# Two attentions of a transformer stack on TensorE: score and mask matmuls in smaller array tiles, masking in the contraction, and a new call order

## The reference

```python
# x: (8, 256, 128); everything float32
x = x + layernorm(attn(layernorm(x)))     # 16 heads of 8, 4 key/value heads, causal over 256 tokens
x = x + layernorm(ffn(layernorm(x)))      # two layers of local attention and a gated MLP
# attn: q = x@Wqa@Wqb, k/v = x@Wkva@Wkvb, rope on q and k
scores = jnp.einsum('bqhd,bkhd->bhqk', q, k) * scale
scores = jnp.where(causal, -jnp.inf, scores)
out = jnp.einsum('bhqk,bkhd->bqhd', softmax(scores), v) @ Wout + bout
# each layer of ffn: 8 heads of 64, window 64; token shift, l2norm of q and k, xpos rotation
sim = jnp.einsum('bhwid,bhwjd->bhwij', q, k)          # 64 queries against 128 keys
mask = (i < j) | (i > j + 64) | (j == -1)
x = x + (softmax(where(mask, -max, sim)) @ v) @ wo
x = x + (a * gelu(g)) @ w2 + b2                        # a, g = split(layernorm(shift(x)) @ w1 + b1)
```

## Time and profile before

| | us |
|---|---|
| median of 3 runs (lowest, highest) | 502.34 (502.02, 503.59) |
| the profiled execution, its own time | 504.87 |
| its span, first to last instruction | 503.0 |
| PE busy | 467.1 (93%) |
| DVE busy | 376.5 (75%) |
| ACT busy | 343.7 (68%) |
| POOL busy | 317.0 (63%) |

### The profile page before, as it was taken

How to read it: one execution, slowest core, us unless ns; L and a number is a source line. 1 busy time by engine, 2 the same in 40 slices (tenths; PEclk the granted TensorE clock), 3 DMA queues, 4 the chain that set the end, 5 groups by cost and what they waited for, 6 DMA issues and landing times.

```text
span 503.0 us, 14088 instructions
## 1 busy us (share of the span) xinstructions
PE 467.1 (93%) x5472; PEld 292.8 (58%) x5472; DVE 376.5 (75%) x725; ACT 343.7 (68%) x906; POOL 317.0 (63%) x250
## 2 busy tenths in 40 slices
PE   8879999999999898999799989999999899999992
PEld 6555766675664566756545656655654466556641
DVE  3835684678775986899868796958888879868576
ACT  1135656565567788878886797788674888998632
POOL 2322251445979899779989865868669966564011
PEclk9979999999999989999999989999999999999996
DMA  5022022000001001010000010100010001011002
GB/s 149 2 91 89 7 45 46 4 3 3 4 2 44 3 1 22 3 43 3 1 22 2 22 23 1 24 1 22 3 22 21 20 5 23 2 23 22 2 8 76
DMA packets 13453, 11.43 MB, mean 23 GB/s; under 512 B 4194, under 2 KB 10700, under 8 KB 13388
## 3 DMA queue, kind: packets, MB, share of 16 engines
q1 hardware_dynamic: 13388, 10.54, 8.3%
HBM read 5.16 MB, written 1.05 MB: 12 GB/s over the span
## 4 chain that ended last, share of the span: by engine, by line
PE 71%; ACT 9%; DVE 8%; issue 6%; POOL 5%; DMA 1%; SPq 0%; ACTq 0%; DVEq 0%; POOLq 0%
PE bank L464 10%; PE bank L558 8%; PE bank L679 7%; PE bank L638 5%; ACT bank L1268 5%; PE bank L648 5%; PE bank L567 5%; PE bank L500 4%; PE bank L693 4%; PE bank L619 4%; PE bank L578 3%; PE bank L477 3%; PE bank L596 3%; PE bank L600 2%; POOL r_qk L2346 2%
## 5 line engine op out<-in xcount | busy, mean ns | idle before, releaser
L2346 POOL TENSOR_TENSOR r_qk<-ss,minus_half 128x16 f32<-128x16 f32 x32 | 93.7, 2929 | 2.7
L1268 ACT ACTIVATE bank<-bank,mn_b 128x128 f32<-128x128 f32 x256 | 88.8, 368 | 4.1 <-DVE mn_b L1818 4.0
L2339 POOL TENSOR_TENSOR rc<-rc,rs 128x1024 f32<-128x1024 f32 x32 | 75.5, 2360 | 21.3 <-DVE rs L1810 21.3
L1751 DVE TENSOR_REDUCE mx_a<-bank 128x2 f32<-128x512 f32 (+1 forms) x96 | 61.7, 685 | 32.2 <-PE bank L477 31.8
L1221 ACT ACTIVATE pT_k<-bank 128x512 f32<-128x512 f32 x96 | 52.9, 597 | 38.4 <-PE bank L477 38.4
L558 PE MATMUL bank<-wqkv,xS 128*128 128x512 f32 x128 | 62.6, 612 | 1.7 <-issue 1.1
L464 PE MATMUL bank<-qT_a 32*128 32x128 f32 (+1 forms) x1024 | 57.4, 351 | 6.6 <-DVE mx_a L1751 3.3
L2353 POOL TENSOR_TENSOR rc<-rc,r_qk 128x1024 f32<-128x1024 f32 x32 | 60.8, 1902 | 2.8
L1268 ACT ACTIVATION_READ_ACCUMULATOR bank<-bank,mn_b 128x1 f32 x256 | 60.2, 235 | 0.0
L464 PEld LDWEIGHTS bank<-qT_a 32*128 32x128 f32 x1024 | 41.0, 192 | 19.8 <-issue 9.5
L679 PE MATMUL bank<-yfT,w 128*128 128x512 f32 (+1 forms) x96 | 49.1, 612 | 0.3 <-ACT v_b L1251 0.3
(11 more groups left out here) (125 smaller groups left out, 849.7 us busy)
## 6 DMA issues: line engine op xcount, KB each, us to landing
v_b<-v_b SPq DMA_DIRECT2D x32, 128.0 KB, 2.3
wqkv<-in_L_ffn_wqkv_dram SPq DMA_DIRECT2D x2, 768.0 KB, 4.4
out_dram<-pT_k SPq DMA_DIRECT2D x4, 256.0 KB, 2.4
x_all<-in_L_attn_x_dram SPq DMA_DIRECT2D x1, 768.0 KB, 5.0
w<-in_L_ffn_w_dram SPq DMA_DIRECT2D x2, 341.0 KB
wo<-in_L_ffn_wo_dram SPq DMA_DIRECT2D x2, 256.0 KB, 4.6
const<-consts_dram SPq DMA_DIRECT2D x1, 352.0 KB, 4.5
x_all<-in_L_attn_x_dram SPq DMA_DIRECT2D x1, 256.0 KB, 2.8
```

Of the source, the lines that this page charges most:

```text
L1268: m = s.activation(x, x, ACT.Exp, bias=mn_b[:, qt, c, p:p + 1], scale=-1.0, accum_out=sum_b[:, qt, c, p:p + 1])
L1751: v.tensor_reduce(mx_a[:, qt, h0:h0 + nh], full(src).rearrange("p (h k) -> p h k", h=nh), AX.X, ALU.max).then_inc(S("a_mx"), 1)
L2339: g.tensor_tensor(rc[:, k % 2, :, :], rc[:, k % 2, :, :], rs[:, k % 2, :, :], ALU.add).then_inc(S("b_add"), 1)
L2346: g.tensor_tensor(r_qk[:, n, :], ss[:, n, :], minus_half[:, :], ALU.pow).then_inc(S("b_r"), 1)
```

## The change

- `a_quad`: each score matmul is cut into four of 32 stationary columns, so that the call uses sixteen tiles of 32x32 (four row groups by four column groups). The four float32 matmuls of a head become sixteen, with the same moving columns.
- The causal mask between different blocks of 32 tokens goes into the contraction: query block i of 32 tokens has ones in rows 9 + i to 15 of its group, key block i > 0 has -1e30 in row 8 + i, so that a product -1e30 is added where the key block is later. At the start of the program POOL writes these ones and values into `qk_a` with 14 small memsets (7 for the ones, 7 for the values), and the first `a_turn` waits for them. The mask matmuls then cover only the diagonal 32x32 blocks: sixteen for each call, in 32x32 tiles, of 64 or 128 columns.
- The mask constants shrink from 256 to 32 float32 columns, so that one load at the start is smaller.
- `b_scores` of even units uses 64x64 tiles as well: 16 matmuls of 64 stationary columns for 8 of 128.
- The order of the calls of every engine, and the banks, are new. TensorE's list has one call more: `busy` appears seven times for six.

```diff
-    for c0, m in ((C_MQ, np.where(k > q, NEG, 0)), (C_MK, np.where(q > k, NEG, 0))):
-        c[:, c0:c0 + PARTS // 2] = packed(m)
-        c[:, c0 + PARTS // 2:c0 + PARTS] = packed(np.roll(m, PARTS // 2, 0))
+    q32, k32 = q % ROWS, np.arange(ROWS)[None, :]
+    c[:, C_MQ:C_MK] = packed(np.where(k32 > q32, NEG, 0))
+    c[:, C_MK:C_MB] = packed(np.where(q32 > k32, NEG, 0))
...
             def a_turn(b, c, dst, *free):
 
+                if b == 0:
+                    t.wait_ge(S("a_pads"), 1)
...
                 for i in range(nh):
-                    for n, (queries, v) in enumerate(pairs):
+                    for o in range(0, PARTS, ROWS):
+                        for n, (queries, v) in enumerate(pairs):
+                            for c in range(2):
+                                dst = full(banks[2 * n + c])[o:o + ROWS, i * w:(i + 1) * w]
...
+                                own = slice(tile * PARTS + o, tile * PARTS + o + ROWS)
...
+                                t.matmul(dst, left, right, start=(i == 0), stop=False,
+                                         tile_position=(g * ROWS, o), skip_group_check=True)
+
+
+                for n, (queries, v) in enumerate(pairs):
+                    first = w - PARTS if queries else 0
+                    for j in range(PARTS // ROWS):
                         for c in range(2):
...
+                            g = (use_q if queries else use_k)(v, c)[1] // A_GROUP
+                            r, o = slice(g * ROWS, (g + 1) * ROWS), slice(j * ROWS, (j + 1) * ROWS)
...
+                            m = t.matmul(dst[o, :, first + j * ROWS:first + (j + 1) * ROWS], ident_h[r, r],
+                                         (mask_q if queries else mask_k)[r, :].unsqueeze(1).broadcast_to([ROWS, nh, ROWS]),
+                                         start=False, stop=True, tile_position=(g * ROWS, j * ROWS), skip_group_check=True)
...
                 for p in range(PAIRS):
-                    for w in range(qt + 1):
+                    for w in range(2):
...
+                            dst = full(2 * pair + c)[w * WINDOW:(w + 1) * WINDOW, p * PARTS:(p + 1) * PARTS]
+                            q0, k0 = qt * PARTS + w * WINDOW, qt * (w + 1) * WINDOW
+                            t.matmul(dst, qk[r, 0, p, q0:q0 + WINDOW], qk[r, 1, p, k0:k0 + PARTS], start=(p == 0),
+                                     stop=False, tile_position=(c * HD, w * WINDOW), skip_group_check=True)
...
+            for i in range(SEQ // ROWS):
+                n, p = i // (PARTS // ROWS), i % (PARTS // ROWS)
+                r = slice(p * ROWS, (p + 1) * ROWS)
+                if i < SEQ // ROWS - 1:
+                    m = g.memset(qk_a[r, n, 0:A_HEADS, A_D + 1 + i:A_D + SEQ // ROWS], 1.0)
+                if i > 0:
+                    m = g.memset(qk_a[r, n, A_HEADS:A_QK, A_D + i:A_D + i + 1], NEG)
+            m.then_inc(S("a_pads"), 1)
```

More of the change, by code:

```diff
@@ L719, in _ @@
[L719 to L728, removed]
@@ L893, in _ @@
[L893 to L901 removed]
+            a_turn(0, 2, 0, ("w_copied", 2, 2))
+            busy(7, 2, 256)
+            a_quad(0, 0, (1, 6, 5, 2), of("a_xnT_out", 1), of("a_st_out", 0, 0, 3), of("a_rope", 0))
@@ new lines, in _ @@
+            b_v(2, 3, of("a_exp", 6, 4, 12))
+            a_turn_back(5, 4, of("a_exp", 6, 6, 12))
+            a_quad(7, 4, (6, 7, 1, 0), of("a_mx", 7, 6, 12), of("a_exp", 6, 7, 12))
+            b_scores(0, 2, of("a_o", 5))
+            a_quad(7, 5, (3, 2, 1, 0), unit("b_v", 2), of("a_mx", 7, 7, 12), of("a_exp", 6, 9, 12))
+            b_proj(3, 3, of("a_mx", 7, 9, 12))
+            b_turn_qk(1, 1, of("a_mx", 7, 11, 12))
+            a_values(6, 0, 1, of("a_exp", 6, 10, 12))
+            a_values(6, 1, 1)
@@ new lines, in _ @@
+            a_h0(3, 4, unit("b_o", 0))
+            a_quad(8, 2, (2, 3, 5, 0), unit("b_rot", 4), of("a_exp", 7, 4, 12))
+            b_scores(1, 3, of("a_exp", 7, 6, 12))
+            a_out(5, 1, of("a_exp", 7, 7, 12))
+            a_turn_back(6, 2, of("a_exp", 7, 9, 12))
+            b_proj(5, 2, of("a_h0T_out", 3), of("a_exp", 7, 10, 12))
+            a_values(7, 0, 2, of("a_o", 6))
+            a_values(7, 1, 2)
+            b_turn_qk(3, 0, of("a_exp", 7, 11, 12), of("a_yin", 5))
+            b_turn_p(1, 1, of("a_ov", 7, 0, 2))
@@ new lines, in _ @@
+            b_turn_p(8, 0, unit("b_o", 7), group("f_y", 0))
+            b_scores(9, 1, unit("b_trT_out", 9))
+            b_turn_qk(10, 0, unit("b_pT_out", 8))
+            b_out(3, 4, unit("b_rot", 11))
+            a_h0(6, 7, unit("b_p", 8))
+            b_values(8, 3)
+            b_scores(10, 0, unit("b_trT_out", 10))
+            b_turn_p(9, 2, batch("b_x", 3))
+            b_proj(12, 3, unit("b_o", 8), of("a_h0T_out", 6))
+            b_values(9, 1)
+            b_proj(13, 2, unit("b_pT_out", 9))
@@ new lines, in _ @@
+            b_values(12, 0)
+            f_norm_t(2, 3, unit("b_p", 13))
+            b_turn_p(13, 2, unit("b_trT_out", 14))
+            b_scores(14, 0, unit("b_o", 12), chunk("f_gate", 1, 0))
+            b_v(14, 5, unit("b_pT_out", 13))
+            f_plain(1, 0, 7, chunk("f_gate", 1, 1))
+            b_values(13, 1)
+            f_plain(1, 1, 6, group("f_x", 0))
+            b_proj(16, 2, unit("b_v", 14))
+            b_proj(17, 3, chunk("f_act", 1, 1))
+            b_turn_qk(15, 1, unit("b_o", 13), group("f_y", 2))
@@ L1109, in _ @@
-            b_turn_p(25, 3, unit("b_trT_out", 28))
-            b_scores(26, 1, unit("b_rot", 30))
-            f_down(4, 0, 6, unit("b_pT_out", 25))
-            f_plain(4, 2, 7)
+            f_down(1, 0, 1, unit("b_pT_out", 15))
+            f_down(1, 1, 1)
+            f_down(1, 2, 1)
+            b_v(16, 0)
+            b_v(17, 6, unit("b_rot", 18))
+            f_gated(2, 0, 2, unit("b_o", 15))
+            b_proj(19, 0, unit("b_v", 16), group("f_x", 1))
+            f_plain(2, 0, 7)
+            f_gated(2, 1, 5, unit("b_p", 16))
@@ new lines, in _ @@
+            f_down(2, 1, 1)
+            f_down(2, 2, 1)
+            b_proj(22, 2, unit("b_rot", 21))
+            b_turn_p(18, 3, unit("b_trT_out", 20))
+            b_out(8, 1, group("f_x", 2))
+            f_norm_t(3, 3, unit("b_p", 19))
+            b_values(18, 0)
+            b_turn_qk(21, 3, unit("b_pT_out", 18))
+            b_proj(23, 2, unit("b_rot", 22))
+            b_scores(20, 3, unit("b_trT_out", 21))
+            b_turn_p(19, 0, unit("b_o", 18), batch("b_x", 8))
+            f_back_t(3, 3, group("f_y", 3))
@@ new lines, in _ @@
+            b_v(24, 6, chunk("f_act", 3, 2))
+            b_scores(23, 1, batch("b_x", 10))
+            b_turn_p(22, 3, unit("b_v", 24))
+            f_back_t(4, 0, unit("b_o", 21))
+            f_down(3, 0, 5, unit("b_p", 22))
+            f_down(3, 1, 5)
+            f_down(3, 2, 5)
+            b_proj(26, 0, group("f_yT", 4))
+            b_values(22, 2)
+            b_turn_p(23, 3, unit("b_pT_out", 22))
+            b_turn_qk(24, 2, unit("b_o", 22), group("f_x", 3))
+            b_v(25, 3, unit("b_p", 23))
@@ new lines, in _ @@
+            f_down(5, 0, 3, group("f_y", 6))
+            b_out(14, 2, ("last_n", 1, GROUPS))
+            f_down(5, 1, 3)
+            b_turn_p(30, 0, chunk("f_act", 5, 2), group("f_yT", 6))
+            f_gated(6, 0, 5, unit("b_p", 30))
+            f_down(5, 2, 3)
+            b_turn_p(31, 0, unit("b_pT_out", 30))
+            b_values(30, 2)
+            b_values(31, 3)
+            last_t(5, 4, unit("b_o", 30))
+            b_out(15, 0, unit("b_pT_out", 31))
+            f_plain(6, 0, 3, group("f_x", 5))
@@ L2256, in _ @@
             last_shift(6)
+            f_x(7, 7)
+            last_stats(7, 3)
             last_shift(7)
```

2166 lines of the change are left out of this document (1033 added, 1133 removed).

## The result

The changed kernel takes **545.1 us** (median of 4 runs) where the kernel before takes 502.4: a ratio of 1.084, 95% interval 1.080 to 1.088. The forecast was 495, range 485 to 512. The change is 42 us slower, on the side of rivals C and D and far outside the price of C.

A forecast was written before the change was run, and what follows sets the result against it. TensorE was taken to set the pace of the first attention. Its 7.1 us saving plus 0.6 at the end made 7.7, counted as 7 with nine tenths of TensorE's: 495 us as a median, range 485 to 512.

The forecast's parts named there:

- Rival C: `a_quad`: only 25 to 30 records of look-ahead fit, calls 1.6 and 2.2 us; end 508 to 516; chance 0.24.
- Rival D: TensorE: record starts bounded at about 25 to 27 ns each; 53 to 63 us more, up to 565; chance 0.05.
- the small term on the records' queue: TensorE's instruction queue: 29 more packets, 1.1 us each, hide behind TensorE unless one call outruns them; nothing, at most 2 us.
- Look-ahead, rival B: `a_quad`: 48 records of look-ahead, twelve tiles work at once, 3.8 us gained in 48 calls; 495 us, chance 0.38.
- Term 1, changes of shape: TensorE's list: 84 fewer tile-shape changes at 0.093 us each, 7.8 us off if sixteen tiles run together.
- Term 3, masks: `a_quad`: sixteen small masks cheaper than two streamed rounds, 5.1 us off if sixteen tiles run together.
- The new order: All engines' lists: worth only the end's 0.6 us, from `last_stats(6)` ahead of `f_x(7)`, and eight changes of shape.
- POOL's memsets, the filler, the constant load: Memsets 1.5 us, hidden at the start; filler nothing to 0.9 us where TensorE waits; smaller constant load nothing.

The follow-up runs named there:

- order_and_b: Kernel before with the new order and banks and the new local scores, but the old `a_quad` and masks: 492.1 us, ratio 0.978 to before.
- same_tiles: Changed kernel, masking in the contraction kept, but `a_quad` scores and its sixteen diagonal masks in 32x128 tiles: 487.3 us, ratio 0.970 to before.
- calls_alone: TensorE alone, no reference work: series of new and old `a_quad` calls and small matmuls; new calls in a row took 2.05 us (256 columns) and 3.85 (128).
- the padding above: `same_tiles` plus 28 or 56 one-column matmuls adding zeros in each `a_quad`: 505.9 and 548.9 us, for 503.5 before.

## Why the prediction was wrong, step by step

The difference of the change to its control `order_and_b` is 52 us (on two chips), 50.3 in the spans of the profiled runs. In those two traces it divides so: 11 us from the length of undisturbed calls; 26.6 us of TensorE idle by "issue" (27.5 against 0.9); and 8 to 10 us because each of these 31 stops begins while streams still run, some 0.3 us that count as busy (in the stopped call above 1.04 idle for 1.31 between two starts). 2 to 5 us are left unassigned.

- **The step that failed** is the small term on the records' queue: "29 more packets hide behind TensorE unless one call outruns them: nothing, at most 2 us". I had the count right (44 + 29 = 73 packets) and took the packet's own 1.1 us for its price. What counts is how soon the next 256 records can follow: 3.3 to 3.4 us at best. A call of 256 columns has 160 records in 1.5 us, one of 128 has 288 in 1.95, so calls outrun it nearly everywhere. The term measured 35 to 37 us, a few of which are waits of another kind or the packet behind the weights. The condition was written down and never divided out. At 1.1 us a packet the division would just have passed, since the densest calls of the forecast (288 records in 1.32 to 1.50 us) need 256 records in 1.2 us or a little more; what was missing was the 3.3 to 3.4 us, and no row of before holds it. Its closest two packets, 4.0 us apart, only say that so fast a supply had not been seen.
- **Look-ahead, rival B.** "1.32 us for 256 columns and 1.32 to 1.50 for 128" was 1.51 and 1.95: of the gain of 3.8 us a loss of 11. The model let the tiles start at 7 ns in every round. That holds for the first round only (sixteen tiles in 0.10 us, so 60 records *can* be passed over, against my limit of 48, if the four of a matmul stand together as I took them; a trace sorted by start does not show that); later ones start at 16.7 ns, and each return to the first tile has a hole. Rival C's 1.6 and 2.2 us were nearer, with another mechanism.
- **Term 1, changes of shape:** right in direction. Scores run into masks without a gap, and even `b_scores` are 0.18 us shorter (1.43 to 1.25) in most units, twice the 0.093; I had read the 0.12 off a short unit. At the end little is seen of it: 501.8 to 501.5 in the old order, interval through 1, and 493.4 to 492.1 in the new one on two chips, for 16 x 0.093 = 1.5 expected. Neither pair resolves it.
- **Term 3, masks:** sixteen small masks do take less than eight large ones if they stay in the tile shape of the scores: 8.8 us off the calls in `same_tiles`, of which 48 x 0.093 = 4.5 would be the change of shape by the prediction's price.
- **The new order**, priced at "the end's 0.6 us and the eight changes of shape", was worth 8.4 us (501.8 to 493.4). PE's work rose most in the stretch where all engines are near; which of the moved calls did it is not known.
- **POOL's memsets, the filler, the constant load:** nothing of them shows; `same_tiles` has the memsets and is the fastest.
- **Rival D:** a start every 25 ns was right for one tile. In `calls_alone` 64 bf16 matmuls of 32 columns start 25.0 ns apart in the 128x128 tile and, just so, when all 64 use the same 32x32 tile; going round sixteen 32x32 or four 32x128 tiles they start some 8 ns apart. The Trainium skill's floor of about 25 ns ("TensorE: Matmul & The Clock Gate", Part 1) thus agrees for each tile and not for matmuls that go to different ones. It also fits the padding above: its one-column matmuls alternate between two tiles and start in pairs 25 ns apart, 12.5 each. Its 10.6-fold gain for sixteen tiles (Part 3) isn't seen here with 128 columns and two passes, where sixteen tiles do four times the work of four in 1.83 us for 1.01; no run had its 512 columns.

What makes the hole at the return to the first tile was not settled, nor why the next block takes 3.3 us and more when its packet moves in some 1 us.

## What to carry to other kernels

Cutting matmuls into smaller tiles multiplies records, and TensorE's records have two prices of their own: some 4 ns each to start, and a supply of 256 in 3.4 us at best. Before such a change count the records of the densest 3.4 us of TensorE's list. Kernels of this study with up to 204 there lost next to nothing to the supply, apart from the stop behind the weights; in the two with nearly 400 some twenty-seven blocks cost 0.2 to 2.3 us each. Masking in the contraction together with masks in the tile shape of the scores was worth 4.8 us without the small tiles; no run separates the two.

## What was not expected of the hardware

- TensorE's instructions come in blocks of 256 records, and a block can follow the one before after 3.3 us at the soonest (3.33 in the changed kernel, 3.29 with TensorE alone), though the packet moves in 0.9 to 1.5 us. Before, the closest two were 4.0 us apart.
- In a float32 matmul the second pass of one tile does not hold up the first passes of fifteen others (sixteen starts in 0.10 us), but only in the first round.
- 64 float32 matmuls of 32 columns take three times as long in 32x128 tiles as in 32x32 ones (3.77 and 1.22 us), where bf16 ones of both shapes take 0.6.
